# Second queries in buffers of their own, projections in the opening's filling time, first queries sent in two parts

## The chip, the core and the metric

The kernel runs on one core of a Trainium2 chip. The metric is the device time of one execution in microseconds (us); lower is better. The core's engines work side by side, each through its own instruction queue in order: TensorE (PE; its weight loads are PEld), VectorE (DVE), ScalarE (ACT), GpSimd (POOL) and SyncE (SP), which here issues all transfers. They are held together by semaphores alone.

## What is computed

One layer over 8 batch rows of 512 positions and 256 features: layernorm, then attention with 32 query heads in 8 groups that share a key and value head each, within a window of 128 positions either side and with a sink, and beside it a gate.

```python
xn = _layernorm(x, axis=-1)
q = einsum('bqm,muh->bquh', xn, Wq) + bq      # 32 heads of 64; k, v: 8 heads
q = _interleaved_rope(q, cos, sin) * SCALE    # k the same
scores = where(|i - j| <= 128, q k^T, -1e9)   # a sink logit per head is added
s = softmax(scores)[..., :-1] v @ Wo + bo
g = _silu(round_fp8(xn / scale) @ w_ffn + bias)   # scale: largest |xn| over all 8 rows
x = x + s * g
```

## The kernel before

All is computed in f32 precision out of two fp32r parts, a high one and a low one (`_hi`, `_lo`): a projection of a 128 column block is six products of 512 columns (`project`, `project_values`), the scores are two.

The work goes in 64 steps `it`, one for each batch row and key head (group); step -1 is a short one ahead, and each has four slots q, one for each tile of 128 query positions. In step `it`, TensorE multiplies and weighs the scores of group `it`; it projects the queries of group `it + 2`; and one slot behind, it computes the plain score rows of group `it + 1`, of which VectorE takes the maxima (`score_rows` and `maximum`, with `back(it + 1, q, 1)`). Other work has fixed slots: value tiles, keys and transposes by `chunk_at`, the gate's products by `ffn_at`, and VectorE's gate work in `beside`. `heads_at` gives the order of the four heads in a slot.

A group's queries go like this. TensorE projects the even and the odd half into the bank `ring[1]`; ScalarE adds the bias (`even_out`, `odd_out`); GpSimd turns them (`turn_even`, `turn_odd`, `turn_rest`) into `q_first` and `q_second`; ScalarE takes their high parts and GpSimd the low ones (`first_low`, `second_low`); SyncE sends the four parts, 256 KB each, from 128 partitions into 32 partitions each of `qT_full` (`queries_in`, for group 0 `first_queries_in`), and once they are in copies the high half to `qT_high` (`highs_in`, 512 KB). A score row waits for all four parts. The four buffers `q_first`, `q_second`, `q_first_hi`, `q_second_hi` are there once, so `turn_even(a)` waits until the transfers of group a - 1 are in.

SyncE's order in a step: the high copy of group `it + 1`, the keys of group `it + 2` (four transfers `keys_high_in`, two `keys_low_in`), loads, then the queries of group `it + 2`. Ahead of step -1 come the keys and queries of group 0, and a load of batch row 5 into `x_res`.

In the opening the weights come in chunks through spare buffers (`spare`, `chunk_at_first`), and the batch rows too, which VectorE surveys one by one for their statistics and extremes (`survey_spread`, `survey_max`, `survey_min`; `x_at_first` gives each its spare buffer). `warm` and `turn_over` are products that nobody reads. Ahead of step -1 TensorE projects the keys of the first four groups, the queries of group 0 and value tiles 0 to 2; in step -1 the queries of group 1 and 26 `turn_over`; value tile 3 in slot 1 of step 0.

## Time and profile before

| | us |
|---|---|
| median of 3 runs | 1662.32 (1662.12 to 1667.08) |
| profiled execution | 1662.82 |
| its span, first to last instruction | 1661.1 |
| busy: TensorE | 1622.7 (98%) |
| busy: VectorE, GpSimd, ScalarE | 1147.1, 1038.6, 988.0 |
| mean granted TensorE clock | 0.996 of full |

All rows are of the profiled execution, its times from the start of the span. A line in order of time has start, duration, engine, line of the kernel, operation, the tile written and the tiles read, shapes, how many were merged (x), and in brackets the idle time ahead of it with what ended it. "Issue" there means that the profile shows nothing that it waited for. The clock is given as a share of 2.4 GHz; 0.50 is 1.2 GHz. The ends of matmuls are modelled and overlap with the next one: where they follow without idle time, the distance of the starts is the cost.

### The profile page before, as it was taken

The numbers are of one execution on the slowest core, as the hardware profiler recorded it, in microseconds if no ns is written. First come the engines' busy times: TensorE is split into PE (matmuls) and PEld (weight loads), VectorE is DVE, ScalarE is ACT, GpSimd is POOL, SyncE is SP. The second block draws the span as 40 slices with busy tenths as digits, with TensorE's granted clock in tenths as the row PEclk, the third lists the DMA queues.
The fourth block names the chain that finished last, engine by engine and source line by source line (L and its number), as shares of the span: only waits on it lengthen the run. The fifth ranks groups of instructions, "written<-read, shape, count | busy, mean of one in ns | idle before, by whom it ended". The sixth has DMA issues, their size and how long they took to land.

```text
span 1661.1 us, 34148 instructions
## 1 busy us (share of the span) xinstructions
PE 1622.7 (98%) x11203; PEld 1459.4 (88%) x11203; DVE 1147.1 (69%) x3621; ACT 988.0 (59%) x2405; POOL 1038.6 (63%) x1013
## 2 busy tenths in 40 slices
PE   7899999999999999999999999999999999999998
PEld 6688888899898988989889898898989899898987
DVE  7677787666766666766767667676767676766664
ACT  3566555666665665566655666556665566556663
POOL 6677565764756656665656656567566666657551
PEclk9999999999999999999999999999999999999999
DMA  8645445355353445455364454554454445453550
GB/s 236 116 104 106 81 83 99 71 96 99 67 113 71 84 89 88 92 90 90 67 114 81 78 109 65 93 98 77 90 86 84 96 84 98 72 93 70 90 99 14
DMA packets 77279, 150.90 MB, mean 91 GB/s; under 512 B 12720, under 2 KB 25264, under 8 KB 73008
## 3 DMA queue, kind: packets, MB, share of 16 engines
q1 hardware_dynamic: 77104, 148.71, 47.7%
q8 instruction: 92, 1.51, 0.4%
q14 instruction: 83, 0.68, 0.2%
HBM read 18.64 MB, written 4.19 MB: 14 GB/s over the span
## 4 chain that ended last, share of the span: by engine, by line
PE 88%; DVE 4%; issue 3%; ACT 3%; POOL 1%; DMA 1%; SPq 0%; POOLq 0%; DVEq 0%
PE pv_bank L1448 29%; PE ring L1335 13%; PE ring L1406 11%; PE acc L1473 10%; PE score L1432 8%; PE score L1434 8%; PE ring L1458 4%; PE ring L1344 2%; DVE junk L1076 1%; PE ring L1325 1%; PE ring L1378 1%; ACT qT_high L768 1%; ACT prob_all L733 1%; DMA qT_full<-q_first 1%; PE ring L1305 0%
## 5 line engine op out<-in xcount | busy, mean ns | idle before, releaser
L1076 DVE CUSTOM_DVE_ANT_0 junk<-ring,mask,sink 128x384 bf16<-128x384 f32 (+1 forms) x1024 | 558.3, 549 | 288.3 <-PE ring L1406 270.5
L1448 PEld LDWEIGHTS pv_bank<-v,prob_all 128*128 128x128 f32 x5120 | 682.7, 191 | 31.9 <-ACT prob_all L733 11.8
L1448 PE MATMUL pv_bank<-v,prob_all 128*128 128x65 f32 x5120 | 685.9, 265 | 4.7 <-DVE o_norm L1091 2.2
L624 POOL TENSOR_SCALAR_AFFINE_SELECT prob_all<-prob_all 128x512 f32<-128x512 f32 x384 | 252.4, 671 | 443.0 <-ACT prob_all L733 442.4
L733 ACT ACTIVATE prob_all<-score 128x512 f32<-128x512 f32 x640 | 370.4, 596 | 176.9 <-PE score L1434 168.3
L1406 PE MATMUL ring<-kT_high,qT_full 128*128 128x384 f32 (+1 forms) x1024 | 370.0, 361 | 14.7 <-issue 8.3
L1432 PE MATMUL score<-qT_full,kT_high 128*128 128x512 f32 x640 | 263.6, 412 | 0.5
L1434 PE MATMUL score<-qT_high,kT_low 68*128 68x512 f32 x640 | 254.4, 397 | 0.0
L1406 PEld LDWEIGHTS ring<-kT_high,qT_full 128*128 128x128 f32 x1024 | 195.4, 191 | 49.3 <-DVE row_max L1076 14.7
L791 ACT ACTIVATE oT_hi<-ring 128x256 fp32r<-128x256 f32 x256 | 96.5, 377 | 182.4 <-PE ring L1458 181.6
L768 ACT ACTIVATE qT_high<-ring,ident_r 4x256 fp32r<-4x256 f32 x512 | 196.0, 451 | 3.5 <-PE ring L1378 0.3
L1097 DVE TENSOR_TENSOR oT_lo<-ring,oT_hi 128x256 fp32r<-128x256 f32 x256 | 107.7, 421 | 124.1 <-ACT oT_hi L791 122.5
L1473 PE MATMUL acc<-wo_hi,oT_hi 128*128 128x256 f32 x512 | 155.5, 304 | 0.2 <-DVE oT_lo L1097 0.2
L584 POOL TENSOR_TENSOR q_first<-q_first,q_first_hi 128x512 f32<-128x512 f32 x64 | 84.0, 1312 | 114.7 <-ACT q_first_hi L750 114.7
L1473 PE MATMUL acc<-wo_hi,oT_lo 128*128 128x256 f32 x512 | 144.1, 281 | 0.0
L1473 PE MATMUL acc<-wo_lo,oT_hi 128*128 128x256 f32 x512 | 143.3, 280 | 0.0
L1432 PEld LDWEIGHTS score<-qT_full,kT_high 128*128 128x128 f32 x640 | 121.7, 190 | 15.9 <-ACT prob_all L733 1.6
L1335 PE MATMUL ring<-xT_hi,w_hi 128*128 128x512 f32 x316 | 127.2, 403 | 2.2 <-ACT q_even L739 0.8
L1335 PE MATMUL ring<-xT_hi,w_lo 128*128 128x512 f32 x316 | 125.3, 396 | 0.0
L1335 PE MATMUL ring<-xT_lo,w_hi 128*128 128x512 f32 x316 | 124.4, 394 | 0.0
L1434 PEld LDWEIGHTS score<-qT_high,kT_low 68*128 68x128 f32 x640 | 121.3, 190 | 3.0
L1091 DVE TENSOR_TENSOR o_norm<-pv_bank,rden 128x256 f32<-128x256 f32 x256 | 108.6, 424 | 9.3 <-DVE rden L1088 0.5
(167 smaller groups left out, 2540.8 us busy)
## 6 DMA issues: line engine op xcount, KB each, us to landing
qT_high<-qT_full SPq DMA_DIRECT2D x64, 512.0 KB, 4.5
qT_full<-q_first_hi SPq DMA_DIRECT2D x64, 256.0 KB, 5.7
qT_full<-q_second_hi SPq DMA_DIRECT2D x64, 256.0 KB, 5.5
qT_full<-q_first SPq DMA_DIRECT2D x64, 256.0 KB, 4.3
qT_full<-q_second SPq DMA_DIRECT2D x64, 256.0 KB, 4.3
kT_high<-k_first_hi SPq DMA_DIRECT2D x128, 64.0 KB, 2.5
kT_high<-k_second_hi SPq DMA_DIRECT2D x128, 64.0 KB, 2.5
x_res<-in_x SPq DMA_DIRECT2D x11, 512.0 KB, 6.3
```

Of the source, the lines that this page charges most:

```text
L624: nc.gpsimd.affine_select(out=pr, in_=pr, compare_op=ALU.is_ge, fill=0.0, base=0, pattern=[[0, GROUP], [sign, P]], channel_multiplier=-sign) \
L733: nc.scalar.activation(prob[:, q % 2 * 3 + n, :], score[(FIRST[q] + n) % 2][:, :], ACT.Exp) \
L768: last = nc.scalar.activation(qT_high[D:D + NR, s % 2, h, pair * 2 * P:(pair + 1) * 2 * P], ring[2][0:NR, 0:2 * P], ACT.Copy, scale=ident[ ...
L1076: nc.vector.tensor_tensor_reduce(junk[:, h % 2, 0:cols], ring[h % 2][:, 0:cols], mask[:, m0:m0 + cols], 1.0, sink[:, col:col + 1], ALU.add ...
L1091: nc.vector.tensor_tensor(o_norm[:, :, :], pv[:, :, 0:D], rden[:, :].rearrange("p (h a) -> p h a", a=1).broadcast_to([P, GROUP, D]), ALU.m ...
L1097: nc.vector.tensor_tensor(oT_lo[:, q % 2, :], ring[2][:, 0:KT * P], oT_hi[:, q % 2, :].bitcast(F32), ALU.subtract).then_inc(s_oT_lo_done, 1)
L1335: last = nc.tensor.matmul(bank[:, :], w[:, k, col:col + P], xs[:, k, :], start=(n == 0), stop=(n == len(products) - 1))
L1406: nc.tensor.matmul(ring[h % 2][:, 0:cols], qT_full[:, b % 2, h, q * P:(q + 1) * P], kT_high[:, b % 3, k0 * P:k0 * P + cols], start=True, s ...
L1432: nc.tensor.matmul(score[blk % 2][:, :], kT_high[:, c % 3, k * P:(k + 1) * P], qT_full[:, c % 2, :, q * P:(q + 1) * P], start=True, stop=F ...
L1434: nc.tensor.matmul(score[blk % 2][:, :], kT_low[0:D + NR, c % 3, k * P:(k + 1) * P], qT_high[0:D + NR, c % 2, :, q * P:(q + 1) * P], start ...
L1448: last = nc.tensor.matmul(pv[:, h, :], prob[:, q % 2 * 3 + n, h * P:(h + 1) * P], v[:, slot, k, :], start=(n == 0), stop=(n == len(BLOCKS[ ...
L1473: last = nc.tensor.matmul(acc[q // 2][:, (q % 2) * M:(q % 2 + 1) * M], left[:, q % 2, k * P:(k + 1) * P], right[:, col:col + M], start=fre ...
```

## The change

- The queries of group 1 get buffers of their own (`twin_parts`: the two halves of `x_res`, a part of `prob`, and `xq`). `turn_even(1)` waits for the first survey and the first weights' low parts instead of the transfers of group 0; GpSimd's `chunk_low(6)` comes behind group 1's queries; ScalarE takes their high parts in slot 0 of step -1.
- The queries of group 0 are sent in two parts of 256 columns, eight transfers of 128 KB. Rows of tiles 0 and 1 wait for the first four alone.
- The queries of group 1 are sent in the order of group 0 (`second_queries_in`), each without the wait for scores.
- The load of batch row 5 moves from ahead of step -1 to step 0, behind the keys. The spare buffers of batch rows 2 and 3 are swapped, and the load of row 2 waits for a second chunk.
- Value tile 3 and the queries of group 2 are projected in step -1 into other banks; 8 `turn_over` stay there, and 6 come at the step's end.
- The gate work of batch row 0 on VectorE and ScalarE comes about one slot later.

The diff, cut: context and lines that only rename a buffer are left out.

```diff
     if (k, q) == (0, 1):
-        return ("v", n, TILES - 1) if 0 <= n < BATCH else None
+        return ("v", n, TILES - 1) if 1 <= n < BATCH else None
...
+        first_parts = (q_first[:, :], q_second[:, :], q_first_hi[:, :], q_second_hi[:, :])
+        x_res_flat = x_res[:, :, :].rearrange("p t m -> p (t m)")
+        twin_parts = (x_res_flat[:, 0:SEQ], x_res_flat[:, SEQ:2 * SEQ], prob[:, 2, :],
+                      xq[:, :, :].rearrange("p t m -> p (t m)").bitcast(F32))
+        def q_parts(a):
+            return twin_parts if a == 1 else first_parts
...
-        x_at_first = (4, 0, 1, 3, 4, 3, 4)
+        x_at_first = (4, 1, 0, 3, 4, 3, 4)
...
             def queries_in(a, second):
-                    (0, q_first, q_first_hi, s_first_lo, s_qT_first_in)
+                first, second_part, first_hi, second_hi = q_parts(a)
             def first_queries_in():
-                for row, part, ready, done in ((D, q_first_hi, s_first_hi, s_qT_first_in),
-                                               (D + HALF, q_second_hi, s_second_hi, s_qT_second_in),
-                                               (0, q_first, s_first_lo, s_qT_first_in),
-                                               (HALF, q_second, s_second_lo, s_qT_second_in)):
+                parts = ((D, q_first_hi, s_first_hi, s_qT_first_in), (D + HALF, q_second_hi, s_second_hi, s_qT_second_in),
+                         (0, q_first, s_first_lo, s_qT_first_in), (HALF, q_second, s_second_lo, s_qT_second_in))
+                for row, part, ready, _ in parts:
-                    sp.dma_start(qT_full[row:row + HALF, 0, :, :].bitcast(F32), part[:, :]).then_inc(done, 16)
+                    sp.dma_start(qT_full[row:row + HALF, 0, :, 0:2 * P].bitcast(F32), part[:, 0:2 * P]) \
+                        .then_inc(s_qT_half_in, 16)
+                for row, part, _, done in parts:
+                    sp.dma_start(qT_full[row:row + HALF, 0, :, 2 * P:].bitcast(F32), part[:, 2 * P:]) \
+                        .then_inc(done, 16)
+            def second_queries_in(a):
+                first, second, first_hi, second_hi = q_parts(a)
+                for row, part, ready, done in ((D, first_hi, s_first_hi, s_qT_first_in),
+                                               (D + HALF, second_hi, s_second_hi, s_qT_second_in),
+                                               (0, first, s_first_lo, s_qT_first_in),
+                                               (HALF, second, s_second_lo, s_qT_second_in)):
+                    sp.wait_ge(ready, a + 1)
+                    upto(sp, done, Q_IN * a)
+                    sp.dma_start(qT_full[row:row + HALF, a, :, :].bitcast(F32), part).then_inc(done, 16)
             def highs_in(b):
+                if b == 0:
+                    sp.wait_ge(s_qT_half_in, 64)
...
                 if it == 0:
+                    load_first_x(5)
...
-                if real(a):
+                if a == 1:
+                    second_queries_in(a)
+                elif real(a):
...
-            sp.wait_ge(s_w_lo_done, 1)
+            sp.wait_ge(s_w_lo_done, 2)
...
-            sp.wait_ge(s_row_done, 1)
-            load_first_x(5)
...
             def turn_even(a):
-                upto(pool, s_qT_first_in, Q_IN * a)
-                upto(pool, s_qT_second_in, Q_IN * a)
+                if a == 1:
+                    pool.wait_ge(s_row_done, 1)
+                    pool.wait_ge(s_w_lo_done, KT)
+                else:
+                    if a == 2:
+                        pool.wait_ge(s_qT_half_in, 64)
+                    pool.wait_ge(s_qT_first_in, Q_IN * a)
+                    pool.wait_ge(s_qT_second_in, Q_IN * a)
+                first, second, _, _ = q_parts(a)
...
-            chunk_low(6)
             second_low(1)
+            chunk_low(6)
...
             def even_out(a):
-                nc.scalar.activation(q_even[:, :], ring[1][:, :], ACT.Identity,
+                nc.scalar.activation(q_even[:, :], (acc[1] if a == 2 else ring[1])[:, :], ACT.Identity,
             def odd_out(a):
-                nc.scalar.activation(q_odd[:, :], ring[1][:, :], ACT.Identity,
+                nc.scalar.activation(q_odd[:, :], (acc[0] if a == 2 else ring[1])[:, :], ACT.Identity,
             def first_high(a):
-                nc.scalar.activation(q_first_hi[:, :].bitcast(F32R), q_first[:, :], ACT.Copy).then_inc(s_first_hi, 1)
+                if a == 1:
+                    act.wait_ge(s_row_done, 2)
+                nc.scalar.activation(q_parts(a)[2].bitcast(F32R), q_parts(a)[0], ACT.Copy).then_inc(s_first_hi, 1)
             def second_high(a):
+                nc.scalar.activation(q_parts(a)[3].bitcast(F32R), q_parts(a)[1], ACT.Copy) \
...
-                    if q == (1 if it < 0 else 2) and real(a):
+                    if q == 2 and it >= 0 and real(a):
-                    if it == -1 and q == 2:
-                        second_high(a)
...
                         chunk_high(FFN_CHUNK)
+                        first_high(a)
+                        second_high(a)
...
-                    if it in (5, 6) and q == (1 if it == 5 else 3):
-                        ffn_exp(0, it - 5)
+                    if (it, q) in ((5, 2), (7, 1)):
+                        ffn_exp(0, it // 7)
...
-                bank = (pv_bank, acc[0], ring[2], ring[1])[t] if m == 0 else ring[1]
+                bank = (pv_bank, acc[0], ring[2], pv_bank)[t] if m == 0 else ring[1]
...
                         moments_of(1)
                     elif k == 5 and q < 2:
                         normalise(1, x_in, (2 * q, 2 * q + 1))
-                    if (k, q) == (5, 1):
+                    if (k, q) == (5, 2):
                         ffn_clamp(0, 0)
-                    elif (k, q) == (5, 2):
+                    elif (k, q) == (5, 3):
                         ffn_one_more(0, 0)
-                    elif (k, q) == (5, 3):
-                        ffn_invert(0, 0, 0)
-                    elif (k, q) in ((6, 0), (6, 1), (6, 2)):
-                        ffn_invert(0, 0, q + 1)
-                    elif (k, q) == (6, 3):
+                    elif k == 6:
+                        ffn_invert(0, 0, q)
+                    elif (k, q) == (7, 1):
                         ffn_gate(0, 0)
                         ffn_clamp(0, 1)
-                    elif (k, q) == (7, 1):
+                    elif (k, q) == (7, 2):
                         ffn_one_more(0, 1)
+                    elif (k, q) == (7, 3):
                         ffn_invert(0, 1, 0)
-                    elif k == 7 and q > 1:
-                        ffn_invert(0, 1, q - 1)
                 if it == KV and q == 0:
+                    ffn_invert(0, 1, 1)
+                    ffn_invert(0, 1, 2)
+                if it == KV and q == 1:
                     ffn_invert(0, 1, 3)
-                if it == KV and q == 1:
                     ffn_gate(0, 1)
                 if (k, q) in ((0, 2), (0, 3)) and n >= 1:
                     gated(n - 1, q - 2)
...
                 values(0, t)
-            for m in range(2, 4):
-                survey_spread(m)
-                survey_max(m)
-                survey_min(m)
+            survey_spread(2)
+            survey_max(2)
+            survey_min(2)
+            values(0, TILES - 1)
+            survey_spread(3)
+            survey_max(3)
+            survey_min(3)
...
-                    nc.tensor.matmul(acc[1][:, :], ident_r[:, :], xT_hi[:, 0, :], start=True, stop=True)
+                    nc.tensor.matmul(score[0][:, :], ident_r[:, :], xT_hi[:, 0, :], start=True, stop=True)
...
+                elif a == 2:
+                    if odd:
+                        pe.wait_ge(s_v_done, 2)
                 elif odd:
...
-                project(W_Q + (a % KV * 2 + odd) * P, s_q_pe, ring[1] if a else score[odd])
+                project(W_Q + (a % KV * 2 + odd) * P, s_q_pe, {0: score[odd], 2: acc[1 - odd]}.get(a, ring[1]))
...
-                if q == 0 and h == 0:
+                if b == 0 and q == 0 and h == 0:
+                    pe.wait_ge(s_qT_half_in, 64)
+                elif h == 0 and q == (0 if b else 2):
+                if q == 0 and h == 0:
...
-                    if slot == 0 and real(it + 2):
+                    if slot == 0 and it and real(it + 2):
...
-                        pe.wait_ge(s_v_done, TILES * (c // KV) + min(q + 2, TILES))
+                        pe.wait_ge(s_v_done, TILES * (c // KV) + (min(q + 2, TILES) if c else TILES))
...
+                if c == 0 and q == 0:
+                    pe.wait_ge(s_odd_done, 2)
...
-                    if q == 0 and real(it + 2):
+                    if q == 0 and it and real(it + 2):
...
-                    if q == 0 and real(it + 2):
+                    if q == 0 and it and real(it + 2):
-                        turn_over(26)
+                        pe.wait_ge(s_v_done, 1)
+                        project_values(TILES - 1, pv_bank)
+                        queries(2, 0)
+                        queries(2, 1)
+                        pe.wait_ge(s_rope, 5)
+                        turn_over(8)
...
+                        if it == -1 and q == 3:
+                            turn_over(6)
```

## Rows read from the trace of the kernel before

**Rows 1.** The page's first lines: engine busy time, and TensorE's chain
```profile
PE 1622.7 (98%) x11203; PEld 1459.4 (88%) x11203; DVE 1147.1 (69%) x3621; ACT 988.0 (59%) x2405; POOL 1038.6 (63%) x1013
...
PE 88%; DVE 4%; issue 3%; ACT 3%; POOL 1%; DMA 1%; SPq 0%; POOLq 0%; DVEq 0%
```

**Rows 2.** The opening by stage: busy time, instructions, TensorE clock, DMA share, GB/s
```profile
core 0: us, PE busy (x) PEld busy (x) DVE busy (x) ACT busy (x) POOL busy (x), PEclk, DMA share, GB/s
52.70:56.20 3.50, 0.02 (x1) 0.01 (x1) 1.87 (x10) 0.69 (x2) 0.63 (x1) 0.73 0.57 63
56.20:61.00 4.80, 4.78 (x15) 3.82 (x16) 2.08 (x4) 2.13 (x5) 2.58 (x3) 0.50 0.67 150
```

**Rows 3.** TensorE in order of time, 28 to 64 us
```profile
28.36 6.08 PE L1351 MATMUL acc<-xT_hi,ident_r 128*128 128x512 f32 x26
36.77 0.36 PE L1406 MATMUL ring<-kT_high,qT_full 128*128 128x256 f32 x1 [2.33 <-issue]
...
47.24 0.40 PE L1432 MATMUL score<-qT_full,kT_high 128*128 128x512 f32 x1
...
52.32 0.40 PE L1434 MATMUL score<-qT_high,kT_low 68*128 68x512 f32 x1
56.22 0.55 PE L1406 MATMUL ring<-kT_high,qT_full 128*128 128x256 f32 x1 [3.50 <-issue]
...
57.64 0.74 PE L1344 MATMUL ring<-w_hi,xT_hi 128*128 128x512 f32 x1
...
60.31 0.94 PE L1448 MATMUL pv_bank<-v,prob_all 128*128 128x65 f32 x4
...
63.18 0.39 PE L1406 MATMUL ring<-kT_high,qT_full 128*128 128x256 f32 x1
```

**Rows 4.** SyncE's transfers in order of time, 25 to 57 us
```profile
25.69 0.62 SPq L417 DMA_DIRECT2D qT_full<-q_first_hi  x1
...
36.76 0.50 SPq L424 DMA_DIRECT2D qT_high<-qT_full  x1
...
41.79 0.59 SPq L398 DMA_DIRECT2D kT_low<-k_second  x1
45.81 0.58 SPq L407 DMA_DIRECT2D qT_full<-q_first  x1
...
56.18 0.51 SPq L424 DMA_DIRECT2D qT_high<-qT_full  x1
```

**Rows 5.** Transfers issued from 45 to 49 us: median time to landing
```profile
qT_full<-q_first SPq DMA_DIRECT2D x1, 256.0 KB, 4.3
...
qT_full<-q_second_hi SPq DMA_DIRECT2D x1, 256.0 KB, 8.4
```

**Rows 6.** GpSimd and VectorE in order of time around the second queries
```profile
36.84 1.28 POOL L557 TENSOR_TENSOR q_first<-q_even,cos 128x512 f32<-128x512 f32 x1 [4.16 <-DMA qT_full<-q_second]
...
45.74 1.29 POOL L589 TENSOR_TENSOR q_second<-q_second,q_second_hi 128x512 f32<-128x512 f32 x1
...
34.53 1.21 DVE L923 TENSOR_REDUCE x_ends<-prob_all 128x4 f32<-128x1024 f32 x1
...
60.55 0.62 DVE L1061 TENSOR_TENSOR v<-ring,v_bias 128x448 f32<-128x448 f32 x1 [1.93 <-PE ring L1344]
...
73.42 1.40 DVE L908 BATCH_NORM_STATS2 stats<-x_res 128x6 f32<-128x256 f32 x4
```

**Rows 7.** DMA share and GB/s in single microseconds
```profile
28.00:29.00 1.00, 1.00 (x6) 0.83 (x5) 1.00 (x4) 0.44 (x1) 1.00 (x2) 1.00 1.12 127
518.00:519.00 1.00, 1.00 (x9) 1.00 (x9) 0.85 (x4) 0.11 (x1) 0.06 (x1) 1.00 1.09 221
```

**Rows 8.** DMA packets in 2.5 to 5 us, while the first 1 KB rows load
```profile
DMA packets 559, 0.84 MB, mean 335 GB/s; under 512 B 16, under 2 KB 467, under 8 KB 559
```

**Rows 9.** VectorE and TensorE around the first gate work, 187 to 191 us
```profile
187.77 1.50 DVE L997 TENSOR_SCALAR x_late<-gate 128x512 f32<-128x512 f32 x1
...
189.75 1.06 PE L1305 MATMUL ring<-ident_r,x_in 128*128 128x128 f32 x8 [1.15 <-DVE oT_lo L1097]
```

More of the change, by code:

```diff
@@ L400, in queries_in @@
             def queries_in(a, second):
-                row, low, high, ready, done = (HALF, q_second, q_second_hi, s_second_lo, s_qT_second_in) if second else \
-                    (0, q_first, q_first_hi, s_first_lo, s_qT_first_in)
+                first, second_part, first_hi, second_hi = q_parts(a)
+                row, low, high, ready, done = (HALF, second_part, second_hi, s_second_lo, s_qT_second_in) if second else \
+                    (0, first, first_hi, s_first_lo, s_qT_first_in)
                 upto(sp, s_score_pe, NB * (a - 1))
@@ L406, in queries_in @@
                 upto(sp, done, Q_IN * a)
-                sp.dma_start(qT_full[row:row + HALF, a % 2, :, :].bitcast(F32), low[:, :]).then_inc(done, 16)
-                sp.dma_start(qT_full[D + row:D + row + HALF, a % 2, :, :].bitcast(F32), high[:, :]).then_inc(done, 16)
+                sp.dma_start(qT_full[row:row + HALF, a % 2, :, :].bitcast(F32), low).then_inc(done, 16)
+                sp.dma_start(qT_full[D + row:D + row + HALF, a % 2, :, :].bitcast(F32), high).then_inc(done, 16)
             def first_queries_in():
-                for row, part, ready, done in ((D, q_first_hi, s_first_hi, s_qT_first_in),
-                                               (D + HALF, q_second_hi, s_second_hi, s_qT_second_in),
-                                               (0, q_first, s_first_lo, s_qT_first_in),
-                                               (HALF, q_second, s_second_lo, s_qT_second_in)):
+                parts = ((D, q_first_hi, s_first_hi, s_qT_first_in), (D + HALF, q_second_hi, s_second_hi, s_qT_second_in),
+                         (0, q_first, s_first_lo, s_qT_first_in), (HALF, q_second, s_second_lo, s_qT_second_in))
@@ L554, in turn_even @@
                 pool.wait_ge(s_even_done, a)
[L555 to L558 removed]
+                if a == 1:
[7 more added lines that the diff above has]
+                first, second, _, _ = q_parts(a)
+                nc.gpsimd.tensor_tensor(first, q_even[:, :], cos[:, :], ALU.mult).then_inc(s_rope, 1)
+                nc.gpsimd.tensor_tensor(second, q_even[:, :], sin[:, :], ALU.mult).then_inc(s_rope, 1)
             def turn_odd(a):
                 pool.wait_ge(s_odd_done, a)
[L563 removed]
+                first, _, _, second_hi = q_parts(a)
+                nc.gpsimd.tensor_tensor(second_hi, q_odd[:, :], sin[:, :], ALU.mult).then_inc(s_rope, 1)
                 pool.wait_ge(s_rope, 6 * a + 3)
[L565 to L566 removed]
+                nc.gpsimd.tensor_tensor(first, first, second_hi, ALU.subtract).then_inc(s_rope, 1)
             def turn_rest(a):
@@ L571, in turn_rest @@
                 pool.wait_ge(s_rope, 6 * a + 5)
-                nc.gpsimd.tensor_tensor(q_second[:, :], q_second[:, :], q_odd[:, :], ALU.add).then_inc(s_rope, 1)
+                second = q_parts(a)[1]
+                nc.gpsimd.tensor_tensor(second, second, q_odd[:, :], ALU.add).then_inc(s_rope, 1)
             def first_sums():
@@ L583, in first_low @@
                 pool.wait_ge(s_first_hi, a + 1)
-                nc.gpsimd.tensor_tensor(q_first[:, :], q_first[:, :], q_first_hi[:, :], ALU.subtract) \
-                    .then_inc(s_first_lo, 1)
+                first, _, first_hi, _ = q_parts(a)
+                nc.gpsimd.tensor_tensor(first, first, first_hi, ALU.subtract).then_inc(s_first_lo, 1)
             def second_low(a):
                 pool.wait_ge(s_second_hi, a + 1)
-                nc.gpsimd.tensor_tensor(q_second[:, :], q_second[:, :], q_second_hi[:, :], ALU.subtract) \
-                    .then_inc(s_second_lo, 1)
+                _, second, _, second_hi = q_parts(a)
+                nc.gpsimd.tensor_tensor(second, second, second_hi, ALU.subtract).then_inc(s_second_lo, 1)
             def keys_sum(quad):
```

7 lines of the change are left out of this document (1 added, 6 removed).

## The prediction

> **What bounds the kernel now.** The page comes first. TensorE is busy for 98% of the span and stands for 88% of the chain that ended last [rows 1], so from about 61 us on time is saved only by taking work off TensorE or by starting its work earlier. The change touches the opening and the order of VectorE's first gate work; the view to read is the order of time of each engine there. TensorE has two holes. It ends 26 fillers at 34.44 and starts the first score row at 36.77; it ends a score product at 52.72 and starts the next row, the first of head group 1, at 56.22 [rows 3]. "Issue" stands as the cause, which hides a transfer: SyncE, which waits for the same queries, issues the copy to `qT_high` at 36.76 and at 56.18, within 0.05 us of both rows [rows 4]. The table by stage gives the price of the second hole: 3.50 us with nothing running, then 4.8 us in which the granted clock is 0.50, 1.2 GHz instead of 2.4 [rows 2].
>
> **Why the second queries land at 56.2.** GpSimd starts to turn them at 36.84, after 4.16 us of waiting for the transfers that still read the shared buffers. It ends their low parts at 47.03 [rows 6]; the first transfer goes out at 45.81 [rows 4]. The first of the four lands 4.3 us after its issue, at 50.1, and the last must have landed by 56.18 [rows 5, 4]: 10.37 us from first issue to all landed, 2.0 us from one landing to the next.
>
> **Part 1, buffers of their own for group 1.** GpSimd is free at about 30: it can turn the second queries when the first keys' low parts are done. It has eight operations of 1.28 us with a pitch of 1.25 (36.84 to 47.03 [rows 6]), so they end at about 40 instead of 47. Then SyncE is the next bound, not GpSimd. In its program order the copy to `qT_high` and the six key transfers of group 1 stand ahead of the second queries. They start when the first queries have fully landed (36.76) and end at 41.79 + 0.59 = 42.38 [rows 4]. Nothing in the change moves that copy ahead, because it still waits for all parts of the first queries. So the second queries are issued at 42.4 instead of 45.8, are in at 42.4 + 10.4 = 52.8, and row 56.22 starts at about 52.9. Gain: 3.3 us. The bounds are an issue at 42.4 with last landings of 10.0 to 11.0 us: the first queries needed 36.76 - 25.69 = 11.07 [rows 4] behind the keys. So 2.7 to 3.7 us.
>
> **Part 2, the first queries in two parts.** Both parts together move the same 1.05 MB. While four such transfers run, the DMA moves 127 GB/s with its engines full [rows 7]. By bytes the first part (524 kB) needs 4.1 us, and it would be in at about 32.5, ahead of the end of TensorE's filling work. The first score row starts at 34.4 instead of 36.8. That is worth little, since VectorE follows: its surveys end at 35.74, and the value tile now stands among them (0.62 us for seven heads [rows 6], and a short operation for the eighth), so its first maximum starts at 36.6, where it started some 0.5 us behind the row of 36.77. Even these 0.7 us and all that TensorE saves before the second hole end in that hole: they make it longer. I cost the splitting at nothing. Its cover is the whole slack before 52.8, worked out under part 3. SyncE issues four more transfers of 0.62 us, until about 31; the keys' low transfers go behind them and are wanted only by the first score, near 45. The load of batch row 5 into `x_res` leaves its place ahead of step -1 and comes behind the keys of group 2: 52.9 and the 5.6 us from 36.76 to 42.38, 58.5. Its first reader is VectorE's survey, at 73.42 before [rows 6], near 68.8 if all moves with the hole: ten microseconds later.
>
> **Part 3, projections in the filling time.** 18 products (two query halves of group 2, value tile 3) replace 18 of 26 fillers at 28.36, whose pitch is 6.08/26 = 0.23 us: nothing changes in where this stretch ends, 34.4. The six extra fillers at the end of step -1 cost 1.4 us. Away from the main path go, first, the 12 products of the query halves, six ahead of group 0's first score and six behind it: 2.8 us, and some 0.7 of waits beside them. From that score to the end of the stretch, 47.24 to 52.72 [rows 3], 5.5 us become about 3.5. That score moves to about 44.9 (the maxima's pace from 36.6, the fillers), and TensorE is through at about 48.5. It then waits for the second queries until 52.8. So this is 4 us of slack, and neither these 12 products nor the six fillers count. Second, the value tile goes from 57.64 to 60.31 [rows 3], behind the hole: this counts in full, 2.67 us.
>
> **Part 4, what the slow clock takes back.** The hole of about 4.3 us is at least as long as the one before, so I take it that the clock falls again and stays at 1.2 GHz for 4.8 us after the restart [rows 2]. Before, 2.67 us of these held the value tile. Now the weighing and the rows behind it run slow in their place. Between 60.31 and 63.18 TensorE has no idle time [rows 3], so work of 1.3 us at full clock takes twice as long: minus 1.3 us (bounds: nothing if the clock holds, which also gives back 0.8 us on the 1.6 us of scores and rows ahead of the values; 1.6 if all slow time is TensorE's own).
>
> **Part 5, the gate work a slot later.** VectorE clamps the first pair (1.50 us at 187.77), and TensorE stands 1.15 us before its transposes at 189.75, waiting for VectorE's `oT_lo`, which is queued behind the clamp [rows 9]. In the next slot the clamp replaces a shorter add, with a transposition's low parts behind it. I take 0.6 of the 1.15 us; bounds are -0.4 (the stall returns a slot later, in this place or with the second gate in step 7) and 1.5.
>
> **Sum.** 3.3 + 2.7 - 1.3 + 0.6 = 5.3 us. The profiled execution took 1662.82 us with a span of 1661.1; the median of the runs is 1662.32, 0.5 below. 1662.82 - 5.3 = 1657.5, against the median 1657.0.
>
> **What a page says.** The Trainium skill, "DMA: Bandwidth & Descriptors", section "Why small descriptors are slow (HBM only)", says that transfers between SBUF addresses don't pay for small descriptors. By that rule the bytes alone count, and the result is the 1657 above; no row of this trace has a 1 KB packet from SBUF to SBUF. Its section on bandwidth has the opposite advice, to batch transfers up to a MiB, and its fit for one kind of queue (2.0 us and the bytes at 436 GB/s) would make eight transfers of 128 KB one after another 8.0 us longer than four of 256 KB, an estimate from that page. The trace has them overlapping: 2.0 us between landings [rows 5, 4].
>
> **Rival 1, packets cost, not bytes (slower).** A 2 KB packet of the query transfers takes 16 x 2048 B / 127 GB/s = 258 ns on an engine. If that is the price of a packet whatever its size, each half needs 8.3 us, the first queries are all in at 45, and the chain behind (keys, second queries) lands near 61.1: 8.3 us later than in the forecast, so 1665.3. Against it: the 1 KB rows of the first load ran at 559 packets in 2.5 us, 72 ns each [rows 8], and 8 KB packets to twice as many partitions reach 221 GB/s [rows 7], which looks like a limit on bytes into 32 partitions. The point where it decides: 1024 packets over 16 engines are 64 each, so 83 ns above the 129 that the bytes need takes the 5.3 us. Chance 0.07; a partial surcharge (10 to 50 ns, 0.6 to 3.2 us) 0.15, giving 1657.6 to 1660.2.
>
> **Rival 2, the clock holds.** Fillers and rows before the hole may keep it at 2.4 GHz through the hole, or for a part of it. Nothing is taken back: 5.3 + 1.3 + 0.8 = 7.4, so 1654.9. Against it, the same kind of hole dropped it before [rows 2]. Chance 0.15.
>
> **Rival 3, no change.** The load into `x_res` has 10.3 us from its issue to VectorE's survey (58.5 to 68.8). It is 524 kB; the two 524 kB query pairs of 45.81 needed 10.37 us together [rows 5, 4], so alone it should land in time, but it shares the queue with whatever is issued beside it. Where it lands at 73.4, VectorE stands there as late as before, TensorE waits for its maxima, and 4.6 of the 5.3 us are given back: 1661.6. Chance 0.13, with whatever else behind 64 us does not move along.
>
> **How the numbers follow.** The forecast as summed has 0.50, with its own range 1655.5 to 1658.8. About what a measurement can tell from no change is 0.3%, 5.0 us: the limit 1657.3 cuts the likeliest case nearly in half. Faster: 0.15 (rival 2), 0.28 of the 0.50, and 0.04 of the small surcharges, 0.47. Slower than 1667.3 needs rival 1 and a lost gate term: 0.05. The rest, 0.48, is same. The range of 1654.3 to 1662.4 leaves out rival 1 and a little of each end.
>
> **What the profile after would show.** The `qT_high` copies at about 36.8 and 52.9; second queries issued at 42.4; one hole near 48.5 to 52.8 with the clock at 0.50 until about 57.6; first weighing near 55; no hole at 34.4. A second `qT_high` copy later than 54, or a first one later than 38, means packet cost. Wrong would be the forecast above all if that copy comes where I put it and TensorE's work behind it doesn't move by 4.6 to 5 us.

## The result, and the profile after

The changed kernel took 1669.43 us (median of 20 runs, 1662.15 to 1675.49), the kernel before in the same runs 1664.48 (1662.12 to 1671.85). The ratio is 1.0026 with a 95% interval of 1.0014 to 1.0037: 4.95 us slower, where 5.3 us faster was forecast. The profiled execution took 1667.46 us, 4.64 more than the one of before. Three executions in the batches below were slow or far out of line (1746.63 us of the kernel with fillers behind the hole, 5792.98 of the changed kernel timed again, 6378.69 of the kernel before); the ranges leave them out, and they tell nothing of the kernels.

The page of the changed kernel. TensorE is busy for 6.0 us more than in [rows 1], with 12 products fewer:

```profile
PE 1628.7 (98%) x11191; PEld 1468.0 (88%) x11191; DVE 1148.3 (69%) x3621; ACT 988.5 (59%) x2405; POOL 1039.4 (62%) x1013
...
PE 88%; DVE 4%; ACT 3%; issue 2%; DMA 1%; SPq 1%; POOL 1%; POOLq 0%; DVEq 0%
```

The same work that takes longer points at the clock. The list of cores, changed kernel:

```profile
core 0: 1665.7 us, clock 0.989
```

A span of 1665.7 us at 0.989 has 18.3 us of withheld clock, one of 1661.1 us at 0.996 has 6.6 (each figure to 0.8 us, since the mean clock is given to three places). The withheld clock went up by 11.7 us, 7 more than the span did, so by this rough count all else became about 7 us shorter. All 20 executions of the changed kernel have a mean clock of 0.984 to 0.991. The table by stage says where (the columns are those of [rows 2]):

```profile
47.50:50.10 2.60, 0.17 (x1) 0.00 (x0) 2.04 (x10) 0.69 (x2) 0.63 (x1) 0.87 0.41 46
50.10:76.50 26.40, 26.37 (x106) 24.54 (x107) 13.81 (x45) 11.70 (x29) 14.06 (x13) 0.50 0.58 134
76.50:110.00 33.50, 33.38 (x221) 29.75 (x221) 25.68 (x83) 18.38 (x44) 23.15 (x21) 1.00 0.53 116
```

The hole is there, shorter than before, and behind it the granted clock is 0.50, 1.2 GHz, for 26.4 us, where it had been 4.8 [rows 2]. TensorE is busy for 26.37 of them. The kernel before had one more low stretch, which neither its rows above nor the prediction mention: the clock was at 0.50 from 37.2 to 40.6 us. The changed kernel's first trace has none there. The kernel before, by stage:

```profile
36.00:40.00 4.00, 3.23 (x10) 2.46 (x11) 1.93 (x8) 0.00 (x0) 3.16 (x3) 0.65 0.97 231
```

SyncE in order of time, changed kernel:

```profile
24.21 0.62 SPq L427 DMA_DIRECT2D qT_full<-q_first_hi  x1
...
34.01 0.51 SPq L451 DMA_DIRECT2D qT_high<-qT_full  x1
...
39.74 0.58 SPq L442 DMA_DIRECT2D qT_full<-prob_all  x1
...
50.09 0.51 SPq L451 DMA_DIRECT2D qT_high<-qT_full  x1
```

The opening did what it was meant to, and more: the second queries were issued at 39.74 and were in at 50.09, 6.1 us sooner than in [rows 4]. TensorE in order of time, changed kernel:

```profile
47.28 0.39 PE L1480 MATMUL score<-qT_high,kT_low 68*128 68x512 f32 x1
50.13 0.55 PE L1452 MATMUL ring<-kT_high,qT_full 128*128 128x256 f32 x1 [2.46 <-issue]
...
51.87 0.95 PE L1494 MATMUL pv_bank<-v,prob_all 128*128 128x65 f32 x4
...
74.44 0.56 PE L1521 MATMUL acc<-wo_hi,oT_hi 128*128 128x256 f32 x1
...
75.87 0.63 PE L1375 MATMUL ring<-xT_hi,w_hi 128*128 128x512 f32 x1
76.29 0.59 PE L1375 MATMUL ring<-xT_hi,w_lo 128*128 128x512 f32 x1
76.72 0.40 PE L1375 MATMUL ring<-xT_lo,w_hi 128*128 128x512 f32 x1
```

Read the durations down the list: a product of 512 columns takes 0.63 us at 75.87 and 0.40 at 76.72. Weighing, scores, rows and six output products of 256 columns went by for 26 us without the clock coming back, and it came back within the first projection. Before, the value tile with its six products of 512 columns stood right behind the hole, and the fast clock followed it [rows 2, 3]. That tile is what the change moved away.

One measure carries the rest: the time from the first row of group 1 to the first product of the next projection. It was 56.22 to 74.68, 18.46 us, before; it is 50.13 to 75.87, 25.74 us, after. The kernel enters this stretch 6.1 us ahead and leaves it 1.2 us behind.

A second fall is 150 us further on. TensorE, changed kernel:

```profile
225.20 0.28 PE L1421 MATMUL ring<-ident_r,neg_parts 128*4 128x128 f32 x2 [0.84 <-DVE oT_lo L1135]
...
226.03 0.85 PE L1494 MATMUL pv_bank<-v,prob_all 128*128 128x65 f32 x6 [0.32 <-DVE o_norm L1129]
...
228.57 1.38 PE L1494 MATMUL pv_bank<-v,prob_all 128*128 128x65 f32 x6
```

The six weighing products of 0.85 us take 1.38 two slots later. The wait of 0.84 us is for VectorE, which has gate work ahead of `oT_lo`; it is in the trace of before too (0.83 us at 224.70), without a fall. The granted clock is 0.50 from 226.9 to 233.7. Between the copies to `qT_high` of groups 8 and 9 the changed kernel loses 2.9 us (0.65 behind, then 3.51).

### The profile page after: what moved, and what is told of

Same layout as the page of the kernel before. It is cut to its first block, busy times and chain, and to the rows that moved or that the text cites. A ratio compares the mean times of both kernels' runs of the same rounds, so it can differ in the third digit from the quotient of the medians.

```text
span 1665.7 us, 34130 instructions
## 1 busy us (share of the span) xinstructions
PE 1628.7 (98%) x11191; PEld 1468.0 (88%) x11191; DVE 1148.3 (69%) x3621; ACT 988.5 (59%) x2405; POOL 1039.4 (62%) x1013
## 4 chain that ended last, share of the span: by engine, by line
PE 88%; DVE 4%; ACT 3%; issue 2%; DMA 1%; SPq 1%; POOL 1%; POOLq 0%; DVEq 0%
PE pv_bank L1494 29%; PE ring L1375 13%; PE ring L1452 11%; PE acc L1521 10%; PE score L1478 8%; PE score L1480 8%; PE ring L1504 4%; PE ring L1384 2%; PE ring L1365 1%; PE ring L1421 1%; ACT qT_high L806 1%; ACT prob_all L769 1%; DVE junk L1114 1%; DMA qT_full<-x_res 0%; SPq L399 0%
## 5 line engine op out<-in xcount | busy, mean ns | idle before, releaser
L1494 PEld LDWEIGHTS pv_bank<-v,prob_all 128*128 128x128 f32 x5120 | 691.6, 194 | 30.5 <-ACT prob_all L769 11.7
L1494 PE MATMUL pv_bank<-v,prob_all 128*128 128x65 f32 x5120 | 693.6, 267 | 4.3 <-DVE o_norm L1129 2.1
L775 ACT ACTIVATE q_even<-ring,q_bias 128x512 f32<-128x512 f32 x62 | 42.7, 689 | 127.0 <-PE ring L1375 127.0
```

The costliest lines, as they stand in the source:

```text
L1494: last = nc.tensor.matmul(pv[:, h, :], prob[:, q % 2 * 3 + n, h * P:(h + 1) * P], v[:, slot, k, :], start=(n == 0), stop=(n == len(BLOCKS[ ...
```

## The experiments

The theory going in has two halves: the hole drops the clock, and what runs behind the hole decides when it comes back. The first half comes out open, the second shown. The rival: the time is lost elsewhere (the halves, the gate slots, `x_res`), and the clock only goes along. All kernels were timed in five rounds beside the kernel before, whose median was between 1662.66 and 1663.54. A filler is a product of 512 columns into a bank that nobody reads; it adds work and leaves the output as it is.

### Fillers in the hole

```diff
+                    if (it, q) == (0, 1):
+                        fill(11)
                     if not first:
                         row(0)
```

> The changed kernel with 11 fillers (512 columns, nobody reads them, 2.5 us) in the hole ahead of the first row of group 1. Theory (the hole drops the clock, and what follows it, weighing in short products, doesn't bring it back for 26 us): the clock stays at 1.00 from 50 to 76 us and the step behind comes some 10 us sooner than in the changed kernel: 1656 to 1660, ratio to the kernel before 0.994 to 0.998. Rival 1 (the clock's fall has nothing to do with the hole): a low clock in this stretch all the same, 1667 to 1671. Rival 2 (the fillers delay the row): row at 50.1 plus what they overrun, up to 1 us slower.

Measured: 1653.76 us (1651.18 to 1654.84, 6 runs), ratio 0.9937 (0.9921 to 0.9953). TensorE, fillers in the hole:

```profile
49.63 2.73 PE L1396 MATMUL acc<-xT_hi,ident_r 128*128 128x512 f32 x11
52.24 0.36 PE L1457 MATMUL ring<-kT_high,qT_full 128*128 128x256 f32 x1
...
67.19 0.40 PE L1375 MATMUL ring<-xT_hi,w_hi 128*128 128x512 f32 x1
```

And its table by stage:

```profile
52.40:76.00 23.60, 22.89 (x161) 20.48 (x161) 18.86 (x62) 15.54 (x38) 19.05 (x17) 1.00 0.75 180
```

The hole is closed, the clock is 1.00, and row to projection takes 14.95 us instead of 25.74. So 2.6 us of useless products (49.63 to 52.24) in a place where TensorE would have stood still return 10.8 us. The low clock after the hole is the cause of the loss; nothing else was changed. The time is 2.2 us below the expected range; this trace has no second fall near 220 us either.

### Fillers behind the hole, hole left open

```diff
                     maxima_turn()
+                    if (it, q) == (0, 1):
+                        fill(6)
```

> The changed kernel with 6 fillers of 512 columns in the place where value tile 3 stood, behind the hole; the hole stays. Theory (dense products behind the hole brought the clock back in the kernel before): clock low from 49.7 to about 55 to 58 instead of to 76; the fillers cost 2.6 us at the low clock and some 10 come back: about 1660 to 1663. Rival (the length of the low stretch is chance, set by the moment of the hole): low to about 76 as in the changed kernel, and 2.6 us slower than it, 1670 to 1672.

Measured: 1660.56 us (1654.86 to 1665.02, 12 runs), ratio 0.9976 (0.9961 to 0.9991). TensorE, fillers behind the hole:

```profile
48.05 0.39 PE L1457 MATMUL ring<-kT_high,qT_full 128*128 128x256 f32 x1 [1.02 <-DVE row_max L1114]
...
48.65 0.63 PE L1485 MATMUL score<-qT_high,kT_low 68*128 68x512 f32 x1
52.11 0.55 PE L1457 MATMUL ring<-kT_high,qT_full 128*128 128x256 f32 x1 [2.83 <-issue]
...
53.53 2.87 PE L1396 MATMUL acc<-xT_hi,ident_r 128*128 128x512 f32 x6
...
58.33 0.67 PE L1499 MATMUL pv_bank<-v,prob_all 128*128 128x65 f32 x4
58.81 0.37 PE L1457 MATMUL ring<-kT_high,qT_full 128*128 128x256 f32 x1
```

Six products of 512 columns stand where the value tile stood. The clock is back at about 58.6, some 10 us after its fall, instead of 27. Row to projection takes 19.31 us, 2.7 of them the fillers themselves (53.53 to 56.20). The mean clocks agree: 0.993 to 0.998 in eleven executions here, against 0.984 to 0.991 in the 20 of the changed kernel.

The product at 48.65 takes 0.63 us: in this trace the clock had fallen at 48.3, behind the wait of 1.02 us and ahead of the hole, which begins at 49.3. So the hole is not shown to be what drops it.

### The value tile put back

```diff
-        return ("v", n, TILES - 1) if 1 <= n < BATCH else None
+        return ("v", n, TILES - 1) if 0 <= n < BATCH else None
...
-                        project_values(TILES - 1, pv_bank)
...
-                        turn_over(8)
+                        turn_over(14)
```

> The changed kernel with value tile 3 projected in slot 1 of step 0 again, as before, and 6 more fillers in the opening in its place. Theory (moving this tile took away the work that brought the clock back): clock low for about 5 us, row of group 1 at 50.1, as much ahead of the kernel before as there, 6 us: about 1657 to 1660. Rival (chance): 1669 to 1672, the changed kernel and 2.7 us.

Measured: 1657.19 us (1653.99 to 1661.19, 10 runs), ratio 0.9965 (0.9951 to 0.9979). TensorE, value tile back:

```profile
51.67 0.55 PE L1451 MATMUL ring<-kT_high,qT_full 128*128 128x256 f32 x1 [3.51 <-issue]
...
53.09 0.73 PE L1383 MATMUL ring<-w_hi,xT_hi 128*128 128x512 f32 x1
...
58.29 1.00 PE L1493 MATMUL pv_bank<-v,prob_all 128*128 128x65 f32 x8
```

The hole is 1.05 us longer than in the changed kernel, and the kernel is about 10 us faster (ratios 0.9965 and 1.0026). Eight weighing products take 1.00 us at 58.29; in the changed kernel eight at 54.85 took 1.80. Here too the clock fell ahead of the hole, at 47.5, and it was back at 57.8. The mean clocks of all ten executions are 0.994 to 0.998. What made the changed kernel slow is the tile that left its place, not the length of the hole. Doing less work there lost time.

### The kernel before, with its hole filled

```diff
+                    if (it, q) == (0, 1):
+                        turn_over(14)
```

> The kernel before with 14 fillers (3.2 us) in its own hole of 3.5 us. Theory (the hole drops the clock): the clock stays at 1.00 from 56 to 61 and 2.4 us come back, less what the fillers overrun; and the runs spread less: 1660 to 1662, ratio 0.998. Rival (the fall has another cause): no change, ratio 1.000.

Measured: 1660.15 us (1658.63 to 1663.02, 12 runs), ratio 0.9979 (0.9968 to 0.9990). TensorE, before with fillers:

```profile
53.14 3.40 PE L1351 MATMUL acc<-xT_hi,ident_r 128*128 128x512 f32 x14
56.83 0.35 PE L1406 MATMUL ring<-kT_high,qT_full 128*128 128x256 f32 x1 [0.28 <-issue]
```

This prices the low clock of the kernel before: row to projection 16.23 us instead of 18.46, 2.2 us. With the next point it closes the account: 16.23 less the value tile at full clock (57.62 to 59.05, 1.43 us) is 14.8, and fillers in the hole of the changed kernel gave 14.95.

### Gate slots of before, and first queries whole

Both on top of the fillers in the hole, so that the clock is out of it.

```diff
-                    if (k, q) == (5, 2):
+                    if (k, q) == (5, 1):
                         ffn_clamp(0, 0)
...
```

> The changed kernel with 11 fillers in the hole, and the gate work of batch row 0 in its slots of before. Theory (the later slots save the 1.15 us stall at the first transposes of batch row 1): 1.0 us slower than the kernel with the 11 fillers alone, 1654.8, with the whole difference between steps 6 and 8. The prediction's own figure for this part is 0.6. Rival (the gate slots brought the second low clock of the changed kernel, near 227 us): no low clock there in this one, and 2 us faster where the other has it.

Measured: 1654.66 us (1652.05 to 1656.9, 5 runs) against 1653.76 for the fillers alone. Between the copies of groups 6 and 7 it falls back by 0.8 us, the stall of [rows 9]; the medians are 0.9 apart, inside their scatter. The rival expected here is refuted: with the gate work in its old slots the clock is at 0.50 from 216.7 to 223.5 us all the same, so the later slots didn't bring the second fall.

```diff
-                    sp.dma_start(qT_full[row:row + HALF, 0, :, 0:2 * P].bitcast(F32), part[:, 0:2 * P]) \
-                        .then_inc(s_qT_half_in, 16)
...
+                    sp.dma_start(qT_full[row:row + HALF, 0, :, :].bitcast(F32), part[:, :]).then_inc(done, 16)
```

> The changed kernel with 11 fillers in the hole, and the first queries sent whole, in four transfers of 256 KB. Theory (the halves move at some 150 GB/s where whole parts move at 127, so all of the first queries are in 9.8 us after the first issue instead of 11.1): the copies to the high buffer and the row of group 1 come 1.3 us later against the issue of the first queries; 1655.0. The prediction's figure (splitting costs and brings nothing): 1653.8. Rival (packets cost): faster than with halves.

Measured: 1657.49 us (1655.33 to 1658.54, 5 runs). SyncE, first queries whole:

```profile
26.45 0.62 SPq L428 DMA_DIRECT2D qT_full<-q_first_hi  x1
...
37.57 0.50 SPq L446 DMA_DIRECT2D qT_high<-qT_full  x1
...
53.71 0.51 SPq L446 DMA_DIRECT2D qT_high<-qT_full  x1
```

From first issue to all landed is 11.12 us, as before (11.07 [rows 4]); in eight halves it is 9.80 (24.21 to 34.01 in the changed kernel). The halves are 1.3 us faster, and the second queries follow. The trace of this kernel is 1.5 us behind that of the fillers alone at the copies of groups 0 and 1, and 2.1 at that of group 2. It had a fall of the clock at 220 to 227 us besides, worth some 3 us, so the 3.7 us between the medians are too much for the halves. The one execution at a mean clock of 0.998 took 1655.33 us; the four at 0.998 in the first run of the fillers alone took 1653.37 to 1654.09.

### One gate part more in an earlier slot

On top of the fillers in the hole:

```diff
-                    elif k == 6:
+                    elif (k, q) == (6, 1):
+                        ffn_invert(0, 0, 1)
+                        ffn_invert(0, 0, 2)
+                    elif (k, q) in ((6, 0), (6, 3)):
                         ffn_invert(0, 0, q)
```

> The changed kernel with 11 fillers in the hole, and the third part of the first reciprocal one slot sooner, in (6, 1) instead of (6, 2), where VectorE has 3.1 us of gate work in one piece and TensorE stands 0.84 and 0.32 us near 225 us. Theory (this stall drops the clock in some executions, 3 us each time): stall of 0.84 gone, 0.5 to 1 us faster than the kernel with the 11 fillers alone, and fewer runs above its fastest. Rival (the stall moves to slot (6, 1)): no change, 1653.8.

Measured: 1653.79 us (1652.19 to 1660.0, 6 runs). TensorE's wait for `oT_lo` in slot (6, 2) went from 0.83 to 0.73 us only, and the time didn't move. Its profiled execution had no second fall, but that tells nothing: seven traces with waits of 0.83 or 0.84 us there had none either, and the six that fell had waits of 0.84 to 0.87.

### Second queries ahead of the keys

On top of the fillers, whose number in the hole becomes 4, then 1, then 2:

```diff
                     highs_in(b)
+                if a == 1:
+                    second_queries_in(a)
                 if real(t) and t % QUAD:
                     keys_high_in(t)
...
-                if a == 1:
-                    second_queries_in(a)
-                elif real(a):
+                if real(a) and a != 1:
```

> The changed kernel with the second queries sent ahead of the keys of group 1, behind the copy to the high buffer, and 4 fillers in what is left of the hole. Theory (SyncE's order sets their landing, not GpSimd): the row of group 1 starts some 3 us sooner against the issue of the first queries, about 23 us behind it instead of 25.9, the hole closes to about 1 us; 1650 to 1652. Rival 1 (the transfers share the DMA, and what they gain the keys lose): row as late as before, a hole of 1.5 us that the 4 fillers don't cover, the clock falls in some runs, 1654 to 1665.

Measured with 4 fillers: 1654.07 us (1652.62 to 1657.2, 5 runs), ratio 0.9945 (0.9933 to 0.9957). SyncE and TensorE, second queries ahead of the keys:

```profile
25.96 0.62 SPq L427 DMA_DIRECT2D qT_full<-q_first_hi  x1
...
36.29 0.59 SPq L442 DMA_DIRECT2D qT_full<-prob_all  x1
...
47.73 0.50 SPq L451 DMA_DIRECT2D qT_high<-qT_full  x1
...
49.00 1.91 PE L1396 MATMUL acc<-xT_hi,ident_r 128*128 128x512 f32 x4
50.71 0.41 PE L1457 MATMUL ring<-kT_high,qT_full 128*128 128x256 f32 x1
```

The queries are in 21.8 us after the first issue instead of 25.9, but the fillers have become the bound: they start at 49.00, after the queries have landed, and at the slow clock, which set in at 48.0, behind a wait of 1.03 us, and was gone at 51.5, behind the four fillers. Expected were 1650 to 1652.

> The changed kernel with the second queries sent ahead of the keys of group 1, and one filler instead of four in the hole. With four, the row stood behind 1.9 us of fillers at the low clock. Theory (the queries were in at 47.7, the keys close behind at about 48.8 to 49): row about 1 us sooner, 22.9 to 23.5 us behind the first queries' issue instead of 24.8; but nothing holds the clock, low from about 48 for 3 to 26 us: 1655 to 1665, with a wide spread. Rival (a hole of this size doesn't matter): 1652 to 1653.

With one filler: 1654.7 us (1653.04 to 1657.16, 5 runs). The row comes 23.6 us after the first issue (49.41 less 25.83). The low clock that was expected here didn't come: it is 1.00 from 46 to 56 us in this trace, with one filler.

```diff
+                            if (it, q) == (0, 0):
+                                pe.wait_ge(s_even_done, 2)
+                                fill(4)
                             row(3)
```

> The same order of transfers, with 4 fillers in slot 0 of step 0, where TensorE stands 1.0 us for VectorE's maximum ahead of the row of the fourth head, and 2 ahead of the row of group 1. Theory (short holes in slot 0, 0.27, 0.66 and 1.03 us, bring the clock down at 48 together with the last one): clock at 1.00 through the stretch, row about 23 us behind the first queries' issue: 1650 to 1652, the fastest version. Rival: clock falls all the same, 1654 as with four fillers in one place.

With four fillers a slot earlier and two in the hole: 1654.53 us (1652.65 to 1656.69, 5 runs). The row is at 47.75, 23.7 us after the first issue, at full clock. Against the fillers alone (52.24 less 26.26, 26.0) it is 2.3 us sooner, and row to projection takes 15.31 us instead of 14.95; but at the median nothing is left, where 1650 to 1652 were expected. Three counts of fillers, one result. The traces say where the gain goes. This one and that of the fillers alone, timed again, have their first queries issued at the same time (24.04 and 24.03). SyncE, four fillers a slot earlier:

```profile
70.15 0.51 SPq L451 DMA_DIRECT2D qT_high<-qT_full  x1
...
223.98 0.50 SPq L451 DMA_DIRECT2D qT_high<-qT_full  x1
...
253.00 0.51 SPq L451 DMA_DIRECT2D qT_high<-qT_full  x1
```

These are the copies of groups 2, 8 and 9; the other kernel has them at 72.93, 226.27 and 252.22. The lead of 2.8 us is still 2.3 at group 8, and at group 9 it is a lag of 0.8: between them lies a second fall, clock 0.50 from 213.2 to 220.0, that the other trace doesn't have. The trace with one filler has the same fall at 215.0. The other executions fit: their mean clocks are 0.995 to 0.997 with four fillers a slot earlier, 0.997 and 0.998 with the fillers alone. So the earlier queries help, and a second fall takes it back. The trace with four fillers in one place has no second fall and has its last copy 0.9 us ahead of the first one with fillers alone.

### The changed kernel and the best one again

Both unaltered.

> The changed kernel itself, on the same chip as the two others. Theory: low clock for more than 20 us behind the hole in every execution, mean clock 0.984 to 0.991, 1667 to 1671. Rival (its 20 executions were a bad chip or hour): 1657 to 1662.

Measured: 1667.01 us (1664.67 to 1671.93, 11 runs), ratio 1.0020 (1.0011 to 1.0029). TensorE, the changed kernel again:

```profile
52.16 0.55 PE L1452 MATMUL ring<-kT_high,qT_full 128*128 128x256 f32 x1 [2.38 <-issue]
77.89 0.63 PE L1375 MATMUL ring<-xT_hi,w_hi 128*128 128x512 f32 x1
```

25.73 us from row to projection, against 25.74 in the first trace, and mean clocks of 0.986 to 0.990. The long low clock is not chance. When the opening's work starts is: the first queries were issued 2.0 us later here (24.0 to 26.5 in all traces). This trace has three shorter low stretches besides, near 38 to 42, 834 to 840 and 1622 to 1629 us.

> The changed kernel with 11 fillers in the hole once more, as the measure for the two above: 1652 to 1655, mean clock 0.997 to 0.999.

Measured: 1653.76 us (1651.68 to 1655.57, 5 runs), ratio 0.9945 (0.9932 to 0.9958); row to projection 14.89 us. This is the best version: the change with 11 useless products in its hole is about 9 us faster than the kernel before and 13 faster than the change alone.

Against the kernel before with its own hole filled (1660.15), the fair partner, it is 6.4 us faster.

The one measure over all of them (starts in us, from the traces). The last column, when the granted clock was at 0.50 around this stretch, is worked out from its means over single microseconds:

| | row of group 1 | next projection | between | stands behind the hole | clock at 0.50 |
|---|---|---|---|---|---|
| before | 56.22 | 74.68 | 18.46 | value tile | 54.3 to 61.1 |
| before, hole filled | 56.83 | 73.06 | 16.23 | value tile, full clock | never |
| changed | 50.13 | 75.87 | 25.74 | weighing | 49.4 to 76.7 |
| changed, again | 52.16 | 77.89 | 25.73 | weighing | 52.0 to 79.3 |
| fillers behind the hole | 52.11 | 71.42 | 19.31 | six fillers | 48.3 to 58.6 |
| value tile back | 51.67 | 70.70 | 19.03 | value tile | 47.5 to 57.8 |
| fillers in the hole | 52.24 | 67.19 | 14.95 | weighing, full clock | never |
| the same, again | 50.47 | 65.36 | 14.89 | weighing, full clock | never |

Read down the last column, the five kernels with an open hole all lose the clock, three of them within the hole and two ahead of it; the three with fillers in the hole don't. What lies right behind the hole orders the low stretches: about 7 and 10 us with the value tile or six fillers, 27 with weighing. Whether the fall itself comes from the hole or from the shorter waits ahead of it, these runs don't separate.

## Why the prediction was wrong

**Part 1, right in its mechanism, small by 1.3 us and some chance.** From the second queries' issue to their landing it took 10.35 us, against 10.4 forecast, and their issue did hang on SyncE's order. The row came 6.1 us sooner instead of 3.3. Of the 2.8 us more, about 1.5 are the start (first queries issued at 24.21 instead of 25.69), which changes from one execution to the next, and 1.3 the halves.

**Part 2, put at nothing, gave 1.3 us.** The two halves were costed at nothing, by bytes, with a surcharge for packets as the rival. They were faster, and the first landing sets all that follows. The sign "no hole at 34.4" didn't come: TensorE stood 1.73 us ahead of 35.97, waiting for VectorE's maximum, off the path. Rival 1 is refuted: no trace shows a surcharge. DMA in single microseconds, changed kernel:

```profile
28.00:29.00 1.00, 1.00 (x6) 0.84 (x5) 1.00 (x7) 1.00 (x2) 1.00 (x2) 1.00 1.08 137
...
31.00:32.00 1.00, 1.00 (x6) 0.83 (x5) 1.00 (x4) 0.53 (x1) 1.00 (x1) 1.00 1.16 158
```

137 to 158 GB/s stand where [rows 7] has 127; with the queries sent whole again it is 117 to 133 from 29 to 36 us. The rule of the Trainium skill that stood in the prediction ("DMA: Bandwidth & Descriptors", "Why small descriptors are slow (HBM only)") agrees so far as packets of 1 KB cost nothing extra here.

**Part 3, right in its path, too large in its term.** TensorE was through at 47.7 and stood 2.46 us; the value tile left the path. It was credited with 2.7 us, what it took at the slow clock. At full clock it is worth 1.4.

**Part 4 is the step that failed:** "I take it that the clock falls again and stays at 1.2 GHz for 4.8 us after the restart". It fell, and stayed for 26.4. The forecast made row to projection 18.46 - 2.67 + 1.3 = 17.1 us; it took 25.74, 8.6 more. The 4.8 us had been read as a property of the fall. The value tile stood within them, and the change removed it; the prediction even said that the work behind would "run slow in their place", and priced only the 1.3 us of the tile's own slot. Rival 2, the clock holds, had the opposite sign; a fall that lasts longer than before was not among the rivals at all. The Trainium skill, "TensorE: Matmul & The Clock Gate", section "Part 1: The HAM clock gate", has the gate follow how busy TensorE is. By the profile's busy time this stretch doesn't agree: 26.37 of 26.40 us, at the lower level throughout.

**Part 5, right.** 0.6 was taken; the kernel gained 1.0 us between the copies of groups 6 and 7 (1.57 behind, then 0.52), and undoing it cost 0.8.

**Rival 3, refuted.** With the clock held, the fillers in the hole are 8.6 us ahead of the kernel before at the copy of group 2 and 9.3 at the last, so nothing behind 64 us failed to move along.

**The sum.** 1662.82 - 5.3 = 1657.5 was expected of the profiled execution. Add 8.6 for part 4 and 2.9 for the second fall, take off 2.8 for the earlier row and 0.4 for the gate: 1665.8. It took 1667.46; the missing 1.7 us lie in small steps, 0.4 from the projection to the copy of group 6 and 1.1 behind that of group 9, and have no one place. With the clock held by 11 fillers the change is worth 9.2 us at the medians (1653.76 against 1663.0), more than the 7.4 of rival 2. Against the kernel before with its hole filled too it is worth 6.4.

**Open.** What drops the clock between 47 and 55 us: in three traces with an open hole it falls within the hole, in two ahead of it. Why waits of 0.84 and 0.32 us near 220 are followed by a second fall in six of fourteen traces and not in the others; it is this fall that takes back what second queries ahead of the keys win. And what it is in the six products that brings the clock back: the runs show only that it follows them.

## What to carry to other kernels

The length of a slow stretch read from one kernel is not a constant to carry into the next: here it was 4.8 us behind the restart with a value tile there, and 26.4 without. Before work that follows a hole is moved, look what stood in front of the rise, and price the case that without it the clock stays down until the next such work. Where TensorE has a hole of a few microseconds, try products that nobody reads, counted so that they end with the wait: 2.6 us of them in idle time were worth 13 us in the changed kernel, more than its edits are with the clock held (9.2), and 14 of them were worth 2.9 in the kernel before. And a kernel with less work and a longer busy time asks for one look at the mean clock first.

## What the runs showed of the hardware

- At 1.2 GHz TensorE went through 26.4 us of weighing, scores, rows, small transposes and six output products of 256 columns almost without idle time (busy 26.37), and the clock didn't rise; it rose within three products of 512 columns of a projection (75.87 to 76.72). Twice the same, 25.74 and 25.73 us from row to projection.
- With six products of 512 columns behind the hole the clock rose 0.8 us after their end in the kernel before (60.3, 61.1), 2.0 us after it with the value tile back and 2.4 us after it with six fillers.
- Where the clock falls moves. Behind the same waits of 0.27 and 1.02 us it fell at 49.4 and 52.0, within a hole of 2.46 and 2.38 us, and in three other traces at 47.5, 48.3 and 48.0, ahead of what was left of the hole. In all five traces with 11 fillers behind these waits it didn't fall. Waits of 0.84 and 0.32 us stood ahead of a fall in the changed kernel, and 0.83 and 0.32 in the kernel before were followed by none.
- 1.05 MB from 128 into 32 partitions of SBUF took 11.07, 11.12 and 11.44 us in four transfers of 256 KB (three traces), 9.66 to 10.14 in eight of 128 KB (eleven traces). The runs don't tell whether that is the packets' size or the number of transfers under way.
- The opening moves by up to 2.5 us from one execution to the next (first queries issued at 24.0 to 26.5), so a gain there must be read from the issue, not from the start of the span.
